# Multiplications of the identity by resident columns, into PSUM banks that nobody reads, at 19 places of TensorE's program

## What is computed

```python
h = _L0_tok_ref(x, ...)                      # 3-level Haar split, softmax gates, merge
h = concatenate([h, txt], axis=1)            # 8 x 333 x 256
h = h + _L0_attn_ref(_layernorm(h), ...)     # attention, 16 heads
h = h + _L0_ffn_ref(_layernorm(h), ...)      # recurrence over the 8 batches
h = h + _L1_attn_ref(_layernorm(h), ...)     # gated scan
h = h + _L1_ffn_ref(_layernorm(h), ...)      # 3 blocks of quantised weights + low rank
h = h + _L2_attn_ref(_layernorm(h), ...)     # masked attention
h = h + _L2_ffn_ref(_layernorm(h), ...)      # top-1 mixture of 8 experts
h = h + _L3_attn_ref(_layernorm(h), ...)     # causal attention with linear bias
h = h + _L3_ffn_ref(_layernorm(h), ...)      # switch experts with a capacity
```

## Time and profile before

| | us |
|---|---|
| median of 3 runs | 2065.36 |
| lowest and highest | 2063.44, 2066.84 |
| the profiled execution | 2068.74 |
| its span, first to last instruction | 2067.0 |
| TensorE busy in the span | 1769.8 (86%) |
| VectorE, ScalarE, GpSimd busy | 1084.6, 753.2, 552.2 |
| mean granted clock of TensorE | 0.941 |

### The profile page before, as it was taken

One profiled execution on the slowest core, in us unless ns is written; L12 is line 12 of the kernel. 1 busy time (PEld: TensorE's weight loads), 2 busy tenths in 40 slices (PEclk: granted clock), 3 DMA queues, 4 the chain that ended last, 5 costly groups with the idle time before them and its releaser, 6 DMA issues. The chain is left out here.

```text
span 2067.0 us, 33185 instructions
## 1 busy us (share of the span) xinstructions
PE 1769.8 (86%) x10034; PEld 1222.8 (59%) x10034; DVE 1084.6 (52%) x3556; ACT 753.2 (36%) x1859; POOL 552.2 (27%) x728
## 2 busy tenths in 40 slices
PE   4599999996997989978784999968899898885998
PEld 3244444444664767746553999846666666663766
DVE  6477676764226766654544222266666666751111
ACT  1144444451321234422221111166656666632121
POOL 0111010003002122221113333333544445543334
PEclk9899999998997989989996999979999999997999
DMA  5744353518700000040113666360100000003351
GB/s 188 139 92 99 77 107 66 99 22 243 312 0 0 1 1 1 1 163 21 27 27 89 229 215 211 109 176 8 28 22 20 21 21 21 21 21 87 118 171 48
DMA packets 90239, 171.74 MB, mean 83 GB/s; under 512 B 26086, under 2 KB 73417, under 8 KB 82558
## 3 DMA queue, kind: packets, MB, share of 16 engines
q1 hardware_dynamic: 67849, 149.47, 25.8%
q0 software_dynamic: 20480, 18.35, 3.3%
q10 hardware_dynamic: 1764, 2.23, 0.6%
HBM read 111.75 MB, written 61.87 MB: 84 GB/s over the span
## 5 line engine op out<-in xcount | busy, mean ns | idle before, releaser
L2556 POOL TENSOR_SCALAR l_P<-l_P,l_ri 111x111 f32<-111x111 f32 (+1 forms) x256 | 178.1, 713 | 178.4 <-DVE l_ri L2729 178.1
L790 ACT ACTIVATE PT<-psT 111x666 f32<-111x666 f32 x192 | 139.4, 726 | 165.6 <-PE psT L888 165.3
L2814 ACT ACTIVATE l_P<-l_S,l_nm 111x111 f32<-111x111 f32 (+2 forms) x384 | 179.3, 471 | 24.8 <-DVE l_nm L2722 24.5
L687 DVE TENSOR_REDUCE mx<-psS 111x2 f32<-111x666 f32 x192 | 159.6, 847 | 30.1 <-PE psS L873 30.1
L899 PE MATMUL psO<-PT,vS 111*32 111x333 f32 x768 | 147.4, 463 | 0.1
L2972 PE MATMUL l_psP<-ident,l_P 111*111 111x111 f32 x768 | 102.6, 270 | 32.5 <-DVE l_PT L2738 26.7
L2972 PEld LDWEIGHTS l_psP<-ident,l_P 111*111 111x111 f32 x768 | 90.1, 179 | 62.8 <-issue 34.5
L2722 DVE CUSTOM_DVE_ANT_0 l_S<-l_psA,l_am 111x111 f32<-111x111 f32 (+1 forms) x256 | 79.1, 330 | 70.5 <-PE l_psA L2958 64.9
L2338 PEld LDWEIGHTS t_psH<-t_xT,expert_w 128*128 128x128 f32 x896 | 105.8, 194 | 1.3
L2338 PE MATMUL t_psH<-t_xT,expert_w 128*128 128x128 f32 x896 | 105.8, 277 | 0.0
L638 POOL TENSOR_TENSOR low<-raw,high 128x333 f32<-128x333 f32 x32 | 28.6, 894 | 276.9 <-DVE high L699 276.9
(11 more groups left out here) (473 smaller groups left out, 3701.7 us busy)
## 6 DMA issues: line engine op xcount, KB each, us to landing
expert_w<-in_moe_dram SPq DMA_DIRECT2D x36, 1024.0 KB, 5.2
xs_scratch<-zeros SPq DMA_DIRECT2D x27, 896.0 KB, 24.3
c_w<-in_moe_dram SPq DMA_DIRECT2D x16, 1024.0 KB, 7.7
qs<-halves_scratch SPq DMA_DIRECT2D x128, 83.5 KB, 3.2
ks<-halves_scratch SPq DMA_DIRECT2D x112, 83.5 KB, 3.8
halves_scratch<-high SPq DMA_DIRECT2D x32, 167.0 KB, 2.5
halves_scratch<-low SPq DMA_DIRECT2D x32, 167.0 KB, 3.2
h_scratch<-h SPq DMA_DIRECT2D x16, 288.0 KB, 2.4
```

The lines of the kernel that those rows point to most:

```text
L687: v.tensor_reduce(mx[J % 2][:, t, c:c + 65:64], psS[s % 2][0:TT, :, 0:T], AX.X, ALU.max, negate=True).then_inc(max_done, 1)
L790: s_.activation(PT[jp % 2][:, :, a, :], psT[0:TT, :, 0:T], ACT.Exp).then_inc(exp_done, 1)
L2556: r = g.tensor_scalar(Pt, Pt, ri[:, c % 2, 2 * t + half:2 * t + half + 1], None, ALU.mult)
L2814: s_.activation(P[c % 4][:, half, at(t):at(t + 1)], Sm[:, half, at(t):at(t + 1)], ACT.Exp, bias=nm[:, c % 2, i:i + 1], scale=-1.0, accum_o ...
```

## The change

A helper `spin(nc, sh, bank, cols, n)` issues `n` matmuls with the identity as one operand and 512 columns of something that lies in SBUF anyway as the other (an image buffer, a weight matrix), into a PSUM bank whose content nobody reads after. It is called 19 times, with 86 matmuls in all: at the start and at the end of blocks, after `START` in the first attention, and ahead of the last routing steps. Four of the calls stand behind a wait of their own that TensorE's program did not have at that point (`h0_first`, `slot_ready` twice, and `out_filled`); two more name loads that were waited for soon after. VectorE gets one instruction, the memset that fills the 512 columns the first call reads. Nothing is taken out and nothing else is moved.

```diff
@@ -106,6 +106,13 @@
     eng.dma_start(out[WIDE:TT], src[WIDE:TT]).then_inc(landed, 16)
+
+
+def spin(nc, sh, bank, cols, n):
+
+
+    for _ in range(n):
+        nc.tensor.matmul(bank, sh.ident[:, :], cols, start=True, stop=True, skip_group_check=True)
@@ -169,6 +176,7 @@
         h0_half, h0_rest = sem("h0_half"), sem("h0_rest")
+        out_filled = sem('out_filled')
         block = ctx.enter_context(nc.Block())
@@ -278,6 +286,8 @@
             pe.wait_ge(ident_ready, 1)
+            pe.wait_ge(out_filled, 1)
+            spin(nc, sh, psG[0][:, :], out[:, 0:2, :].rearrange("p r c -> p (r c)"), 4)
             pe.wait_ge(wd_in, 16)
@@ -292,10 +302,13 @@
             nc.tensor.matmul(psZ[:, 0:10], group[:, :], dots[:, :], start=True, stop=True).then_inc(summed, 1)
+            pe.wait_ge(h0_first, 16)
+            spin(nc, sh, psG[0][:, :], out[:, 0:2, :].rearrange("p r c -> p (r c)"), 5)
...
             v = nc.vector
+            v.memset(out[:, 0:2, :], 1.0).then_inc(out_filled, 1)
@@ -901,8 +914,10 @@
+            spin(nc, sh, first_bank[7], sh.w[:, 0, :, :].rearrange("p k o -> p (k o)"), 1)
             for n, (kind, j) in enumerate(START[:-1]):
                 piece(kind, j, 0, 0, n)
+            spin(nc, sh, psO[:, :], sh.w[:, 0, :, :].rearrange("p k o -> p (k o)"), 9)
             for s in range(AHEAD):
@@ -922,6 +937,7 @@
                     piece(*tail())
+                    spin(nc, sh, psO[:, :], sh.w[:, 0, :, :].rearrange("p k o -> p (k o)"), 5)
             batches(pe, body)
@@ -1066,6 +1082,7 @@
+            spin(nc, sh, ps[0][:, :], sh.w[:, 0, :, :].rearrange('p k o -> p (k o)'), 3)
             turn(0)
@@ -1111,6 +1128,7 @@
             both(pe, body)
+            spin(nc, sh, ps[0][:, :], sh.w[:, 0, :, :].rearrange('p k o -> p (k o)'), 5)
@@ -1241,6 +1259,7 @@
+            spin(nc, sh, psA[0][:, :], sh.w[:, 0, :, :].rearrange('p k o -> p (k o)'), 1)
             turn(0)
@@ -1268,6 +1287,7 @@
             back(B - 1)
+            spin(nc, sh, psQ[0][:, :], sh.w[:, 0, :, :].rearrange('p k o -> p (k o)'), 5)
@@ -1554,6 +1574,7 @@
+            spin(nc, sh, psY[1][0][:, :], sh.w[:, 0, :, :].rearrange('p k o -> p (k o)'), 1)
             start(0)
@@ -1573,6 +1594,7 @@
                 back(b)
+            spin(nc, sh, psT[0][:, :], sh.w[:, 0, :, :].rearrange('p k o -> p (k o)'), 8)
@@ -2076,6 +2098,7 @@
+            spin(nc, sh, psO[:, :], sh.w_last[:, 0, :, :].rearrange("p k o -> p (k o)"), 2)
             for n, (kind, j) in enumerate(FIRST):
@@ -2140,11 +2163,14 @@
             batches(pe, body)
+            spin(nc, sh, psS[0][:, :], sh.w_last[:, 0, :, :].rearrange("p k o -> p (k o)"), 3)
             for j in range(KT):
...
             piece("rk", 0, B - 1, 1, tail("rk", 0))
+            pe.wait_ge(slot_ready, B)
+            spin(nc, sh, psS[0][:, :], sh.w_last[:, 0, :, :].rearrange("p k o -> p (k o)"), 11)
@@ -2349,6 +2375,8 @@
+            pe.wait_ge(experts.loaded, 16 * E)
+            spin(nc, sh, psY[:, :], experts.w2[:, 0, 0:512], 1)
             turn(0)
@@ -2359,6 +2387,7 @@
                 second(s)
+            spin(nc, sh, psH[0][0][:, :], experts.w2[:, 0, 0:512], 8)
@@ -2930,6 +2959,7 @@
+                spin(nc, sh, last_bank[5], wo[:, 0:2, :].rearrange("p c o -> p (c o)"), 4)
                 pe.wait_ge(row_ready, B)
@@ -3023,6 +3053,8 @@
                     piece(*tail(len(LAST) - 1))
+                    pe.wait_ge(slot_ready, B)
+                    spin(nc, sh, psO[:, :], wo[:, 0:2, :].rearrange("p c o -> p (c o)"), 9)
             batches(pe, body)
@@ -3210,6 +3242,8 @@
                         r.then_inc(h_done, 1)
+                pe.wait_ge(stream.w_in[0][0], 16)
+                spin(nc, sh, psH[3][:, :], stream.w[0][:, 0:512], 1)
                 turn(0, 0, 0)
```

## The result

| | median us | before, same rounds | ratio (95% interval) |
|---|---|---|---|
| the changed kernel | 2055.22 (2044.18 to 2057.67) | 2067.78 | 0.9939 (0.992 to 0.9958) |
| a second time | 2053.21 | 2068.38 | 0.9933 (0.992 to 0.9946) |
| a third time | 2050.36 | 2067.26 | 0.9917 (0.9902 to 0.9932) |

The change makes the kernel faster by 12.6, 15.2 and 16.9 us in the three comparisons. The forecast was 24.4, the time 2041. The first time, 2055.2, lies inside the range of 2024 to 2057 but outside the forecast's own range of 2034 to 2047, and the gain is about half of the one forecast.

The account below looks back on a forecast made before the run. TensorE's program was taken to set most of the time, with pauses paid as idleness and slower work behind. Terms summed to 24.4 us: 2068.74 to 2044.3, less 3.4 for the median, 2041; own range 2034 to 2047, wider range 2024 to 2057.

## What to carry to other kernels

Filling an idle stretch with work that nobody reads gives back at most about half of the busy time in the slow stretch behind the pause, and nothing where the clock falls again before the work comes, or another engine holds that work up. The calls have to end with the pause, since nearly all that is over lands on the path (22.6 of 27.6 us here). When an instruction takes ten times its usual time beside another engine's, look whether its end keeps one distance from the other's end wherever it began: then it was blocked, and the remedy is to move the other engine's work into a gap, not to be earlier. And when parts of a change don't add up, look for a place far from the edits that changed, here a loop that lost its code.

## What was not expected of the hardware

A number of instructions ahead of a loop moved this kernel by 7 to 10 us, with idle times of 1.4 to 2.6 us put down to "issue" and the instruction queue's packets as the only trace of it. And the span of one kernel follows the length of its low-clock time, 226 to 253 us in the kernel before, which falls differently in each execution.
